# Centring before the second norm's projection, moved from VectorE to ScalarE in the end of the third max pool

## The reference, cut to what matters

```
x3 = layernorm(y3 + x, ln3_g, ln3_b)       # end of the third pool, y3 = relu([x, p3] @ Wm3.T + bm3)
x  = x_in + x3                             # residual of the whole network
h  = relu((x - mean(x)) / sqrt(var(x) + 1e-5))
h  = relu(h @ w_in + b_in)                 # first projection of the attention layer
```

## Time and profile before

| | us |
|---|---|
| median of 3 runs | 4991.76 |
| all three | 4991.76, 4986.15, 7978.92 |
| the profiled execution, its own time | 4998.77 |
| its span (first to last instruction) | 4996.9 |

### The profile page before, as it was taken

How to read it: one execution, slowest core, us unless ns; L and a number is a source line. 1 busy time by engine, 2 the same in 40 slices (tenths; PEclk the granted TensorE clock), 3 DMA queues, 4 the chain that set the end, 5 groups by cost and what they waited for, 6 DMA issues and landing times.

```text
span 4996.9 us, 64715 instructions
## 1 busy us (share of the span) xinstructions
PE 2990.6 (60%) x15422; PEld 2152.1 (43%) x15422; DVE 2844.5 (57%) x8700; ACT 1726.9 (35%) x4725; POOL 3230.1 (65%) x3289
## 2 busy tenths in 40 slices
PE   3121189967899788888888888788800007961100
PEld 2011167756777665556555565556700003431000
DVE  6755344445444788877888788787443331124433
ACT  1000069955789443335333353333400003420000
POOL 4767667766767377774777747775067772027776
PEclk7555589988899899999999999999955558985555
DMA  5656566656666433333333333333166662246665
GB/s 179 199 170 218 190 210 224 220 190 193 201 213 221 136 103 105 104 104 96 102 104 104 103 94 103 104 105 95 43 228 205 209 204 88 101 146 205 207 205 190
DMA packets 280170, 776.97 MB, mean 155 GB/s; under 512 B 64641, under 2 KB 103810, under 8 KB 275842
## 3 DMA queue, kind: packets, MB, share of 16 engines
q0 software_dynamic: 157104, 429.21, 30.7%
q1 hardware_dynamic: 122706, 343.62, 18.0%
HBM read 455.64 MB, written 316.93 MB: 155 GB/s over the span
## 4 chain that ended last, share of the span: by engine, by line
PE 25%; POOL 14%; DMA 11%; issue 8%; DVE 5%; ACT 2%; DVEq 1%; POOLq 0%; ACTq 0%; SPq 0%
POOL HC L508 11%; PE PS L1314 8%; PE PS L1306 5%; PE PS L1240 3%; DMA X<-table,idx_src 3%; PE PS L1008 3%; DMA HC<-table,idx_src 3%; DMA HC<-table_typ,run_typ 2%; DMA HC<-table_rel,run_rel 2%; POOL HC L484 2%; POOL X L484 1%; DVE work L1931 1%; PE PS L1295 1%; PE PS L1403 1%; DVE W L1923 1%
## 5 line engine op out<-in xcount | busy, mean ns | idle before, releaser
L1744 DVE SCALAR_TENSOR_TENSOR HC<-HC,run_rst 128x256 f32<-128x256 f32 x1890 | 917.6, 486 | 1195.0 <-DMA HC<-table,run_max 526.0
L508 POOL DMA_INDIRECT HC<-table,run_max x1113 | 1098.1, 987 | 450.7 <-issue 305.5
L484 POOL DMA_INDIRECT HC<-table,idx_src x648 | 643.7, 993 | 352.4 <-DMA table<-B 155.8
L1115 PE MATMUL PS<-AM,ring 128*128 128x256 f32 x3000 | 731.0, 401 | 102.2 <-ACT ring L718 63.4
L484 POOL DMA_INDIRECT X<-table,idx_src x600 | 602.7, 1004 | 182.9 <-issue 127.7
L1115 PEld LDWEIGHTS PS<-AM,ring 128*128 128x128 f32 x3000 | 585.1, 200 | 247.9 <-DVE HC L1744 101.1
L1306 PE MATMUL PS<-AM,work 128*128 x3744 | 651.6, 285 | 22.0 <-DVE score L1931 20.5
L1987 DVE SCALAR_TENSOR_TENSOR HC<-HC,fcol,PS 128x257 f32 x1248 | 586.2, 470 | 102.6 <-PE PS L1314 93.2
L508 POOL DMA_INDIRECT HC<-table_typ,run_typ x391 | 378.7, 968 | 394.6 <-DMA table_typ<-HC 275.7
L1148 PE MATMUL PS<-ident,HC 128*128 128x128 f32 x10 | 3.4, 444 | 1002.4 <-DVE HC L1744 1002.4
L508 POOL DMA_INDIRECT HC<-table_rel,run_rel x391 | 378.1, 967 | 289.1 <-DMA table_rel<-AM 170.3
(11 more groups left out here) (261 smaller groups left out, 4390.2 us busy)
## 6 DMA issues: line engine op xcount, KB each, us to landing
prefix<-HC SPq DMA_DIRECT2D x485, 512.0 KB, 3.3
table_typ<-HC SPq DMA_DIRECT2D x18, 1024.0 KB, 3.8
HC<-table,run_max POOLq DMA_INDIRECT x1113, 3.2
HC<-table,idx_src POOLq DMA_INDIRECT x648, 2.8
X<-table,idx_src POOLq DMA_INDIRECT x600, 2.8
HC<-table_rel,run_rel POOLq DMA_INDIRECT x391, 2.8
HC<-table_typ,run_typ POOLq DMA_INDIRECT x391, 2.8
table_typ<-AM SPq DMA_DIRECT2D x6, 1024.0 KB, 3.8
```

What stands on the lines that cost most here:

```text
L484: pool.indirect_dma_start(held(t)[:, 0:D], None, table, bass.IndirectOffsetOnAxis(ap=idx_src[:, t:t + 1], axis=0)).then_inc(landed[t % AHE ...
L508: pool.indirect_dma_start(run_slot(k), None, src, bass.IndirectOffsetOnAxis(ap=run_idx[s[1]][:, j:j + 1], axis=0)).then_inc(landed[k], 16)
L1115: last = nc.tensor.matmul(PS[:, (2, 5)[c % 2], 0:D], quads[:, (QUADS * x + g) % 4, b % 4, :], A[:, b, :], start=(b == 0), stop=(b == BLOCK ...
L1744: V.scalar_tensor_tensor(run_slot(k), run_slot((j - 1) % SLOTS), run_rst[:, j:j + 1], fresh, fade, join).then_inc(pooled, 1)
```

## The change

For the third pool only, `centre` leaves VectorE. ScalarE does it in one activation per block, as `Identity(scale * X + shift)` with scale and shift read from one column each, one value per node. VectorE computes the shift, `-mean * scale`, with one more instruction on a 128x1 column, which waits for the reciprocal. ScalarE's loop gets one more turn, and the two steps behind the centring run one turn later than before (L761 for block i-5 instead of i-4, L765 for block i-7 instead of i-6). The loops of TensorE, and the order of everything else on VectorE, are unchanged. A new tile `shift_of` (25 columns) is added.

```diff
+        shift_of = sb("shift_of", [P, BLOCKS])
@@ ScalarE, third pool's end
+                    def centre_rows(b):
+                        act.wait_ge(scale2_made, b + 1)
+                        if b >= TRS:
+                            act.wait_ge(turned2, u0 + BLOCKS + b - TRS + 1)
+                        nc.scalar.activation(stage_in[:, b % TRS, :], X[:, b, :], ACT.Identity, bias=shift_of[:, b:b + 1],
+                                             scale=scale_of[:, 1, b:b + 1]).then_inc(centred, 1)
-                    for i in range(BLOCKS + 7):
+                    for i in range(BLOCKS + 8):
...
                         if s[2] == 3 and 0 <= i - 3 < BLOCKS:
                             root(n, i - 3, second=True)
                         if s[2] == 3 and 0 <= i - 4 < BLOCKS:
-                            b = i - 4
+                            centre_rows(i - 4)
+                        if s[2] == 3 and 0 <= i - 5 < BLOCKS:
+                            b = i - 5
                             act.wait_ge(turned2, u0 + BLOCKS + b + 1)
...
-                        if s[2] == 3 and 0 <= i - 6 < BLOCKS:
-                            b = i - 6
+                        if s[2] == 3 and 0 <= i - 7 < BLOCKS:
+                            b = i - 7
@@ VectorE, invert(second=True)
-                    V.reciprocal(scale_of[:, 1, b:b + 1], spread_of[:, 1, b:b + 1]).then_inc(scale2_made, 1)
+                    link(V.reciprocal(scale_of[:, 1, b:b + 1], spread_of[:, 1, b:b + 1]))
+                    V.scalar_tensor_tensor(shift_of[:, b:b + 1], means[:, 1, b, 0:1], -1.0, scale_of[:, 1, b:b + 1],
+                                           ALU.mult, ALU.mult).then_inc(scale2_made, 1)
@@ VectorE, third pool's end
-                                    if 0 <= i - 2 < BLOCKS:
-                                        b = i - 2
-                                        centre(n, b, X[:, b, :], stage_in[:, b % TRS, :], u0 + BLOCKS + b - TRS + 1 if b >= TRS else 0, second=True)
```

## The result

The kernel after takes 5003.84 us (median of 7 runs, 4998.6 to 5011.99), the kernel before in the same comparison 4990.18. The ratio is 1.0031 with a 95% interval of 1.0019 to 1.0043, so 15.5 us longer (9.5 to 21.5): small against 2%, but clear of noise. The two medians lie 13.7 us apart; the ratio leaves out a run of 7978.92 us that the median before counts. The forecast was 14.2 us longer and 5006.

What follows compares the result with a forecast made beforehand. TensorE's own work was taken to set the 2.71 us turn. Steady turns 11.0, fill 1.2 and drain 1.9 made 14.2 us, added to the runs' median 4991.76 for 5006, range 4991 to 5024.

Steps and rivals of the forecast that it cites:

- What bounds the kernel: Third-pool stage: TensorE's own work sets the 2.71 us turn; VectorE needs 2.51 and waits 0.20 before each residual.
- VectorE is not relieved: VectorE's turn: link and shift offset the removed centring; 2.51 goes to about 2.6 us, booked as zero.
- The activation: ScalarE's new centring with scale and bias from columns: 0.61 us long, 0.50 from its start to the next.
- The ring: ScalarE's and TensorE's steps wait for each other within one turn: 3.36 us instead of 2.71, 0.65 more; chance 0.80.
- The sum: Whole stage: 17 turns by 0.65 give 11.0, the start 1.2, the end 1.9, together 14.2 us longer.
- Fill: Stage's start: first transposed stage_in 0.94 us later, two turns up to the steady part some 0.3, together 1.2.
- Drain: Five turns after the last gathered block: ScalarE's same distances give 1.9 us more, bounds 0.6 and 3.3.
- Not slower: Rival: L765 gets out in time for the old pace, TensorE stays full, kernel takes 4992 us; chance 0.13.
- Table loads: Rival: Identity in another table than Sqrt, two loads a turn at 1.283 us, kernel 5070 us; chance 0.01.
- The clock: Rival: with TensorE 81% full the stage runs at 1.2 GHz, 25 turns cost 68 us, kernel 5060; chance 0.03.
- What would show it: Profile signs: 3.36 us turns, TensorE idle about 0.26 and 0.4 a turn, VectorE idle longer than 0.20, clock 1.00.

Runs made afterwards that it cites:

- e3: Kernel before with VectorE's centring in this stage cut to one column of 256; 2.71 us a turn, one run of 4991.10 us.
- e4: Kernel after with the centring activation as a copy scaled by a constant, no column operands; 3.08 us a turn, one run of 5007.12 us.
- e1: Kernel after with L765's step back at its old turn (block i-6 instead of i-7); 3.01 us a turn, ratio to before 1.0019.
- e2: Kernel before, centring still on VectorE, with only ScalarE's L761 and L765 steps one turn later; 2.90 us a turn, ratio to before 1.0009.
- e7: Kernel after with VectorE's shift moved behind the second statistics; 3.24 us a turn, one run of 4995.79 us.
- e5: Kernel after with TensorE's loop staggered by one more turn; 2.71 us a turn, ratio to before 1.0001.
- e6: Kernel after with TensorE's loop one turn longer and VectorE's shift behind the second statistics; 2.71 us a turn, ratio to before 0.9997.
- e8: Kernel before, centring on VectorE, with ScalarE's two steps and TensorE's loop each one turn later; 2.71 us a turn, ratio to before 1.0002.

## Why the prediction was right

- **What bounds the kernel.** Right: with TensorE full, 0.14 us less on VectorE in each turn changed nothing (e3). The 0.20 us of waiting stands before 12 of the 17 residuals only, 2.4 us in all.
- **VectorE is not relieved.** Right. From the reciprocal to the statistics is 0.24 us now (I took 0.30), the aggregate starts 0.46 after the statistics as in the earlier trace rows, and VectorE needs 3.24 - 0.70 = 2.54 us, between the 2.51 of before and the 2.6 forecast. A 0.40 us instruction was removed and VectorE has no less to do; what it covered came to light.
- **The activation.** 0.588 us long and 0.49 apart, against 0.61 and 0.50 from the earlier trace rows. The estimate of 0.585 and 0.49 from the figures of the Trainium skill ("ScalarE: Activation LUTs", section "What ACT_TABLE_LOAD costs") was the nearer one, and the 93 ns that it gives for a pointer operand agree with the 92 ns of e4.
- **The ring.** Right in every link. Predicted 3.36, measured 3.24. The mis-sized link is the last on ScalarE's side: L765 to the bias row was taken as 0.50 from the earlier trace rows and is 0.43. In the earlier trace rows the bias row stood at the head of the last block alone, its weight load at 1728.46 and its matmul only 0.07 later; in the steady turn load and matmul start together. The remaining 0.05 is spread over the other links, each within 0.02 of its row. VectorE's aggregate was to be ready 0.29 before the second root; it was 0.25.
- **The sum.** 17 turns: 9.0 measured, 11.0 forecast. Fill: 1.65 against 1.2. Drain: 1.70 against 1.9. The stage is 12.35 us longer, forecast 14.2; the kernel by the ratio 15.5 (9.5 to 21.5). The fill came near by luck. Its 1.65 is made of three parts: the fifth gathered block comes 0.66 earlier in the stage (7.55 against 8.21 us), for the most part since the clock rose earlier; the first centred block follows it 0.90 later than before, forecast 0.94; and from there to the eighth gathered block it takes 1.41 more (7.96 against 6.55), forecast 0.3, for the most part since the clock fell (last section), which the sum did not have. Between the two profiled executions the spans differ by 9.1 only (5006.0 and 4996.9), since other stages scatter by some microseconds. What of the 15.5 lies outside the stage, if anything, these runs don't settle, so that the kernel came within 1.3 us of the forecast is luck as well.
- **The rivals.** Not slower: out, TensorE waits twice in each turn. Table loads: out, no load between the activations of the stage, with `Identity` among them and `Sqrt`; by the Trainium skill, "ScalarE: Activation LUTs", section "Table sets: the hidden batching unit", identity is in every set, and this trace agrees. The clock: 1.00 in the steady part, but see below.
- **What would show it.** TensorE's gaps were forecast as 0.26 and 0.4. By the starts of matmuls, the turn shown against the earlier trace rows, they are 0.19 (from the weights' matmuls to the transpose 1.05 against 0.86) and 0.33 (from the transpose to the bias row 0.55 against 0.22), sum 0.52. The longer wait of VectorE, 0.70, came as said.

## What to carry to other kernels

Where engines run fixed lists tied by semaphores, the cost of a moved instruction is not its duration but the rings it joins: follow from one instruction of the bounding engine through the other lists back to it, add start-to-start distances, and compare with the turn. An engine that is half idle can hold such a ring; its idle time then stands in one piece, before the step that the bounding engine releases. If a step is added to a helper's list, give the engine that waits for it one more turn of stagger: here that bought back all 0.53 us a turn without removing anything. Follow every ring, also those that are just shorter than the turn: shorten the longest, and the next one, here through VectorE (e1, e2), gives the pace.

## What the runs showed of the hardware that was not expected

The clock did fall, not in the steady turns but in the fill. After the change TensorE had nothing to do for 2.27 us before the first centred block, and what follows ran at about half the clock; before, the same gap was 1.37 us and the clock stayed. After, then before:

```profile
1665.03 0.68 PE L1013 MATMUL PS<-ident,work 128*128 128x128 f32 x2 [2.27 <-ACT work L751]
...
1665.00:1667.00 2.00, 1.97 (x7) 1.79 (x8) 1.93 (x8) 0.83 (x4) 1.55 (x2) 0.52 0.44 131
```

```profile
1665.00:1667.00 2.00, 1.72 (x10) 1.45 (x10) 2.00 (x10) 0.95 (x3) 1.45 (x2) 1.00 0.33 82
```

The granted clock was 0.52 from 1665 to 1667 us and 0.63 in the next two, so the engine was at its 1.2 GHz level for most of it. In e1 the same gap was 2.27 us too; the clock was still at 1.00 when the block came, and 0.63 from 1655 to 1659. In e7 the gap was 2.06 and the clock fell at once, but in e4 it was 2.09 and the clock stayed. The two microseconds behind the gap, e7 first, then e4:

```profile
1651.27:1653.27 2.00, 2.00 (x7) 1.78 (x8) 1.72 (x8) 0.98 (x4) 1.70 (x2) 0.54 0.40 123
```

```profile
1664.18:1666.18 2.00, 1.95 (x10) 1.45 (x10) 1.93 (x10) 0.74 (x3) 1.69 (x2) 1.00 0.43 131
```

In the runs with a gap of 1.37 us or less (before, e2, e3, e5, e6, e8) it stayed at 1.00. So the fall goes with the long gap, but the gap's length alone does not decide it, and these runs don't show what else does. A late first item of a pipeline can so cost more than its own delay: from the fifth gathered block to the eighth the kernel after takes 11.90 us and e4 10.29, and 0.5 of the 1.6 between them is e4's shorter activation in three turns, which leaves an estimate of about 1 us for the clock.
